# Router logits with the router as the stationary operand, turned by token in small products

## The reference

```
router_logits = x_flat @ w_router                 # 2048 x 256 times 256 x 8
top_vals, top_idx = top_k(router_logits, 2)
probs = softmax(top_vals)
h = square(relu(x_flat @ w_fc[e]));  y = h @ w_proj[e]
out = sum over the two experts e of a token of probs * y
```

## Time and profile before

| | us |
|---|---|
| median of 3 runs | 308.31 (307.42 to 308.64) |
| the profiled execution | 309.08 |
| its span | 307.3 |
| TensorE busy | 286.2 (93%), 1846 instructions |
| VectorE busy | 196.0 (64%), 467 instructions |
| ScalarE busy | 170.5 (55%), 359 instructions |
| GpSimd busy | 149.4 (49%), 132 instructions |

### The profile page before, as it was taken

The page is one execution under the profiler, slowest core; times in us unless marked ns, Lnnn a source line. Parts: engine busy times, 40 slices in busy tenths (PEclk is TensorE's granted clock), DMA queues, the critical chain, the costliest instruction groups (busy, mean ns, idle before and its releaser), DMA issues.

```text
span 307.3 us, 5659 instructions
## 1 busy us (share of the span) xinstructions
PE 286.2 (93%) x1846; PEld 253.6 (83%) x1846; DVE 196.0 (64%) x467; ACT 170.5 (55%) x359; POOL 149.4 (49%) x132
## 2 busy tenths in 40 slices
PE   5798999999899899999999998999999999799992
PEld 5787788887778789888988987989988999688881
DVE  2785999988967977865546689455546455513332
ACT  0679659797657835444666544356565555422320
POOL 3863101003472023776676687558766667637400
PEclk9799999999999999999999999999999999989998
DMA  6999980017984001244344434343444344429998
GB/s 172 360 365 377 373 323 0 0 11 208 202 213 65 0 20 36 55 69 71 53 71 69 68 57 70 53 69 55 73 69 71 63 65 65 54 33 152 192 198 282
DMA packets 33356, 36.92 MB, mean 120 GB/s; under 512 B 5168, under 2 KB 30512, under 8 KB 33296
## 3 DMA queue, kind: packets, MB, share of 16 engines
q0 software_dynamic: 13840, 17.20, 34.6%
q1 hardware_dynamic: 16560, 17.25, 16.8%
q10 hardware_dynamic: 2928, 2.10, 2.1%
HBM read 24.68 MB, written 13.96 MB: 126 GB/s over the span
## 4 chain that ended last, share of the span: by engine, by line
PE 74%; DVE 13%; ACT 6%; issue 4%; DMA 1%; POOL 0%; DVEq 0%; ACTq 0%; POOLq 0%
PE ps L366 62%; PE ps L586 5%; PE ps L434 5%; DVE cum L983 2%; ACT h L749 2%; DVE gu L1127 2%; DVE Wpj_lo L1122 2%; DMA X<-in_L_attn_x_dram 1%; DVE guT_lo L1132 1%; ACT X L695 1%; DVE h2T_lo L1003 1%; DVE gi L986 1%; PE ps L380 1%; DVE hT_lo L950 1%; DVE X L1140 1%
## 5 line engine op out<-in xcount | busy, mean ns | idle before, releaser
L1364 POOL DMA_INDIRECT xg<-xh_dram,gather_u x39 | 46.6, 1196 | 55.7 <-DVE picks L1157 46.3
L1373 POOL DMA_INDIRECT acc_dram<-yb,gather_u x39 | 62.2, 1596 | 16.4 <-issue 8.8
L366 PE MATMUL ps<-h2T_lo,Wgu_hi 128*128 128x512 f32 x128 | 43.1, 397 | 0.0
L366 PE MATMUL ps<-h2T_hi,Wgu_hi 128*128 128x512 f32 x128 | 41.1, 402 | 1.3 <-DVE h2T_lo L1003 0.9
L366 PE MATMUL ps<-h2T_hi,Wgu_lo 128*128 128x512 f32 x128 | 39.8, 392 | 0.0
L366 PE MATMUL ps<-Wd_hi,guT_hi 128*128 128x256 f32 x128 | 36.5, 285 | 3.3 <-DVE guT_lo L1132 3.3
L1127 DVE TENSOR_TENSOR gu<-gu,ps 128x512 f32<-128x512 f32 x32 | 21.9, 685 | 27.2 <-PE ps L366 25.2
L366 PE MATMUL ps<-Wd_hi,guT_lo 128*128 128x256 f32 x128 | 36.2, 283 | 0.0
L366 PE MATMUL ps<-Wd_lo,guT_hi 128*128 128x256 f32 x128 | 36.1, 282 | 0.0
L1174 DVE TENSOR_TENSOR aT_lo<-ps,aT_hi 128x256 fp32r<-128x256 f32 x39 | 16.5, 424 | 29.0 <-ACT aT_hi L797 24.8
L769 ACT ACTIVATE gu<-ps 128x512 f32<-128x512 f32 x32 | 19.0, 595 | 24.5 <-PE ps L366 23.6
(11 more groups left out here) (178 smaller groups left out, 677.2 us busy)
## 6 DMA issues: line engine op xcount, KB each, us to landing
X<-acc_dram POOLq DMA_DIRECT2D x8, 512.0 KB, 11.0
acc_dram<-zero SPq DMA_DIRECT2D x1, 2176.0 KB, 17.4
X<-in_L_attn_x_dram SPq DMA_DIRECT2D x4, 512.0 KB, 7.4
Wgu_raw<-in_L_attn_w_gate_up_dram SPq DMA_DIRECT2D x4, 512.0 KB, 9.3
Wfc_raw<-in_L_ffn_w_fc_dram SPq DMA_DIRECT2D x4, 512.0 KB, 12.5
xh_dram<-X ACTq DMA_DIRECT2D x4, 512.0 KB, 7.5
Wpj_raw<-in_L_ffn_w_proj_dram SPq DMA_DIRECT2D x4, 512.0 KB, 4.7
out_dram<-X SPq DMA_DIRECT2D x3, 512.0 KB, 5.5
```

The costliest lines, as they stand in the source:

```text
L366: return nc.tensor.matmul(dst, lhs, rhs, start=start, stop=stop, skip_group_check=group)
L1364: pool.indirect_dma_start(out=xg[i % XG][:, :], out_offset=None, in_=xh_dram, in_offset=bass.IndirectOffsetOnAxis(ap=gather_u[:, i:i + 1], ...
L1373: pool.indirect_dma_start(out=acc_dram[i % 2], in_=yb[i % YB][:, :], in_offset=None, compute_op=ALU.add, out_offset=bass.IndirectOffsetOnA ...
```

## The change

`logits(c)` now has `Wr_two` as the stationary operand and all 512 tokens of hT as the moving one: two products of 16 columns by 512 (k = 0, 1) and two of 8 by 512, in one group, 4 in all. The result is by expert: 16 partitions (hi-weight sums in the first 8, lo-weight sums in the others), 512 tokens. A new ScalarE `take_logits(c)` copies it to `by_expert` in SBUF (a place that the feed-forward uses later). A new TensorE `turn_logits(c)` multiplies, for each tile j, by_expert's 16x128 as the stationary operand by `fold` (16x8, two identities of 8 above each other), which both transposes and adds the two halves; operands are plain float32. VectorE's `take_logits(c)` copies these 128x32 to `logit`, once per chunk. All results use bank 7 from its first column, so that logits(c) waits for VectorE's copy of c-1, and ScalarE's copy of c waits for the turning of c-1. `fold` is made by one VectorE addition near the start. `top_two` waits for all four copies. Where each step stands in the queues is in the diff.

```diff
--- before.py
+++ after.py
@@ -144,6 +144,8 @@
         guT_at = room(8 * KB)
         gain = [put(f"gain{b}", [P, K, S], F32, at)
                 for b, at in enumerate((cum_at, cum_at, Wpj_hi_at + 8 * KB, Wpj_hi_at + 12 * KB))]
+
+        by_expert, fold = put("by_expert", [P, S], F32, guT_at), put("fold", [P, E], F32, guT_at + 2 * KB)
         guT = [(put(f"guT{u}_hi", [P, S], F32R, guT_at + 4 * KB * u),
                 put(f"guT{u}_lo", [P, S], F32R, guT_at + 4 * KB * u + 2 * KB)) for u in range(2)]
 
@@ -207,7 +209,9 @@
         xh_ready, xh_half = [sem(f"xh_ready{b}") for b in range(B)], sem("xh_half")
         xh_stored = [sem(f"xh_stored{b}") for b in range(B)]
         xT_done, hT_hi, hT_split, wr_hi, wr_split = sem("xT_done"), sem("hT_hi"), sem("hT_split"), sem("wr_hi"), sem("wr_split")
-        logit_done, logit_copied = sem("logit_done"), sem("logit_copied")
+        logit_done, logit_taken, logit_turned, logit_copied = (sem("logit_done"), sem("logit_taken"), sem("logit_turned"),
+                                                               sem("logit_copied"))
+        fold_ready = sem("fold_ready")
         q2_ready, q_ready = sem("q2_ready"), sem("q_ready")
         zero_row, zero_stored = sem("zero_row"), sem("zero_stored")
         x_copied = sem("x_copied")
@@ -386,15 +390,24 @@
                 pe.wait_ge(hT_split, K * (c + 1))
                 if c == 0:
                     pe.wait_ge(wr_split, 1)
+                else:
+                    pe.wait_ge(logit_copied, c)
+                for k in range(K):
+                    product(ps[0:2 * E, LOGIT, :], Wr_two[:, k, :, :].rearrange("p h e -> p (h e)"), hT[c][0][:, k, :],
+                            k == 0, False, True)
+                for k in range(K):
+                    last = product(ps[0:E, LOGIT, :], Wr_two[:, k, 0, :], hT[c][1][:, k, :], False, k == K - 1, True)
+                last.then_inc(logit_done, 1)
+
+            def turn_logits(c):
+
+                pe.wait_ge(logit_taken, c + 1)
+                if c == 0:
+                    pe.wait_ge(fold_ready, 1)
                 for j in range(J):
-                    t = J * c + j
-                    for k in range(K):
-                        rows_hi, rows_lo = (hT[c][h][:, k, j * P:(j + 1) * P] for h in range(2))
-                        product(ps[:, LOGIT, t * 2 * E:(t + 1) * 2 * E], rows_hi,
-                                Wr_two[:, k, :, :].rearrange("p h e -> p (h e)"), k == 0, False, True)
-                        last = product(ps[:, LOGIT, t * 2 * E:t * 2 * E + E], rows_lo, Wr_two[:, k, 0, :],
-                                       False, k == K - 1, True)
-                last.then_inc(logit_done, 1)
+                    last = nc.tensor.matmul(ps[:, LOGIT, j * E:(j + 1) * E], by_expert[0:2 * E, j * P:(j + 1) * P],
+                                            fold[0:2 * E, :], start=True, stop=True)
+                last.then_inc(logit_turned, 1)
 
             def aiv(b, n):
 
@@ -530,17 +543,21 @@
             logits(0)
             transpose_x(1)
             aiv(0, 4)
+            turn_logits(0)
             aiv(0, 5)
+            logits(1)
             transpose_x(2)
             aiv(1, 0)
-            logits(1)
+            turn_logits(1)
             aiv(1, 1)
+            logits(2)
             transpose_x(3)
             aiv(1, 2)
-            logits(2)
+            turn_logits(2)
             aiv(1, 3)
             logits(3)
             output_projection(0, 0)
+            turn_logits(3)
             output_projection(0, 1)
             aiv(1, 4)
             aiv(1, 5)
@@ -713,6 +730,12 @@
                 act.wait_ge(router_loaded, 16)
                 A.activation(Wr_two[:, :, 0, :], Wr[:, :, :], ACT.Copy).then_inc(wr_hi, 1)
 
+            def take_logits(c):
+                act.wait_ge(logit_done, c + 1)
+                if c:
+                    act.wait_ge(logit_turned, c)
+                A.activation(by_expert[0:2 * E, :], ps[0:2 * E, LOGIT, :], ACT.Copy).then_inc(logit_taken, 1)
+
             def decay(b, r):
                 act.wait_ge(aiv_done, 6 * b + r + 1)
                 if b == 3:
@@ -818,6 +841,7 @@
             decay(0, 1)
             normalise_x(1)
             store_xh(0)
+            take_logits(0)
             input_gate(0, 0)
             input_gate(0, 1)
             split_h(1)
@@ -826,11 +850,14 @@
             gains(0)
             normalise_x(3)
             store_xh(2)
+            take_logits(1)
             split_h(2)
             store_xh(3)
+            take_logits(2)
             split_h(3)
             decay(1, 0)
             decay(1, 1)
+            take_logits(3)
             weights_hi(3)
             input_gate(1, 0)
             input_gate(1, 1)
@@ -1004,14 +1031,13 @@
                                            in1=h2T[b % 2][0][:, k, :].bitcast(F32), op0=ALU.mult,
                                            op1=ALU.subtract).then_inc(h2T_split, 1)
 
-            def take_logits():
-                dve.wait_ge(logit_done, B)
-                two = ps[:, LOGIT, 0:2 * T * E].rearrange("p (t h e) -> p t h e", h=2, e=E)
-                chain.step(V.tensor_copy(logit[:, :, :], two[:, :, 1, :]))
-                V.tensor_tensor(logit[:, :, :], logit[:, :, :], two[:, :, 0, :], ALU.add).then_inc(logit_copied, 1)
+            def take_logits(c):
+                dve.wait_ge(logit_turned, c + 1)
+                V.tensor_copy(logit[:, J * c:J * (c + 1), :].rearrange("p t e -> p (t e)"),
+                              ps[:, LOGIT, 0:J * E]).then_inc(logit_copied, 1)
 
             def top_two():
-                dve.wait_ge(logit_copied, 1)
+                dve.wait_ge(logit_copied, B)
                 te = [P, T, E]
                 rank_te = rank8[:, None, :].to_broadcast(te)
                 work = logit
@@ -1181,6 +1207,7 @@
             split_router()
             statistics(2)
             dve.wait_ge(consts_ready, 1)
+            V.tensor_tensor(fold[0:2 * E, :], ident[0:2 * E, 0:E], ident[0:2 * E, E:2 * E], ALU.add).then_inc(fold_ready, 1)
             V.tensor_copy(lane16[:, :], lane_i[:, :])
             V.tensor_copy(token[:, :], token_i[:, :])
             chain.step(V.tensor_copy(lane[:, :], lane_i[:, :]))
@@ -1190,17 +1217,20 @@
             normalise_x(2)
             gated_value(0, 0)
             split_h(1)
+            take_logits(0)
             gated_value(0, 1)
             scales()
             signal(0, 0)
             signal(0, 1)
+            take_logits(1)
             split_h(2)
             cumulate(0, 0)
             recur(0, 0)
+            take_logits(2)
             cumulate(0, 1)
             split_h(3)
             recur(0, 1)
-            take_logits()
+            take_logits(3)
             top_two()
             add_residual(0, 0)
             add_residual(0, 1)
```

## The result

The changed kernel takes 311.94 us (median of 4 runs, 311.05 to 312.92), the kernel before 308.08 in the same comparison: ratio 1.0127, 95% interval 1.009 to 1.0164. It is 3.9 us slower; 3.2 more had been forecast, from the median of 308.31 known then to 311.5. The profiled execution took 312.02 us, its span is 310.3.

The account below looks back on a forecast made before the run. TensorE was taken as three quarters of the chain, with little room between engines at the edit. Waits making the count 3.2 us late took the profiled 309.08 to 312.3, or 311.5 us on the median; range 309.4 to 314.4.

Parts of the forecast that it names:

- The cost of a turn: TensorE, per chunk: four f32 products standing as eight instructions 0.11 us apart, 0.89 us; ends 0.24 and 1.7.
- The product part: TensorE, per chunk: 4 products with 512 moving columns take 0.91 us in place of 16 taking 1.70.
- Wait 1: TensorE waits at turn_logits(1) from 29.5 us for ScalarE's copy behind normalise_x(3); VectorE's split_h(2) ends at 33.2 instead of 32.0.
- Step 2 and 3: VectorE waits 0.7 us for turn_logits(2), with recurrence work behind it; output projection starts at 42.6 instead of 40.41 us.
- Step 4: turn_logits(3) comes behind half the projection: top_two starts at 45.6 us, +4.4; the count is at 49.95, 3.2 later.
- What arrives at the end: After the count, VectorE falls back from 4.4 us late to TensorE's lateness; everything behind ends 3.2 us late.
- rival D: The 3.2 us delay is there at 50 us but given back before 110 us: some 308.5 us; 8%.
- rival A: TensorE's clock falls at 42.6 us, slowing the projection's first half before turn_logits(3): +1.7, 313.2 us; 25%.
- one of my signs of being wrong: A granted clock of 0.50 between 40 and 50 us was listed among signs that the forecast was wrong.
- my sum: Whole kernel: profiled execution of 309.08 us plus 3.2 gives 312.3; put on the median, 0.77 lower, 311.5 us.
- Rival B: Turns are cheap, 0.03 us an instruction, or ScalarE is early: only +1.3, 309.6 us; 15%.
- Rival C: TensorE's issue time sets the end: no stop at turn_logits(1) and cheap turns give -2.2 us, 306.1; 7%.

Follow-up runs that it names:

- turn by transposes: Changed kernel with copies and last turn reordered; each turn made four transposes, VectorE adding the halves in one reduction, fold gone: 308.39 us, ratio 1.0003.
- two experiments, one at each of them: Each against the changed kernel: ScalarE's copy of chunk 1 ahead of normalise_x(3), 310.94 us; VectorE's copies of chunks 1 and 2 behind the splits, 309.61 us.
- the busy wait: Changed kernel plus 16 small keep_clock products in TensorE's queue in front of logits(3): 310.83 us, ratio 1.0089 to the kernel before.
- the products alone: Changed kernel without turns, ScalarE's copies, three of VectorE's four copies, logits(c)'s wait for the previous copy and fold; routing by meaningless logits: 308.29 us, ratio 0.9984.
- ScalarE's copy early: Changed kernel with ScalarE's take_logits(1) moved ahead of normalise_x(3): 310.94 us, ratio 1.0094 to the kernel before.
- the turns doubled: Changed kernel with the four products of each turn_logits issued twice, same result: 314.97 us, ratio 1.0203 to the kernel before.

## Why the prediction was right, point by point

Right in sign and size: +3.2 forecast, worked out on the path and put on the median of 308.31; +3.9 and +2.9 measured in two comparisons. By its steps, counted from the first product of logits(0), at 20.65 us before and 19.47 after:

- *The cost of a turn*: 0.89 us taken; 0.99 in the trace (23.72 - 22.73). The product part 0.92 (20.39 - 19.47), 0.91 taken. So TensorE's work does hardly change, by 0.2 us per chunk: page part 1 gives PE 286.2 us busy before and

```profile
PE 286.2 (92%) x1830; PEld 248.9 (80%) x1830; DVE 195.9 (63%) x470; ACT 172.7 (56%) x363; POOL 149.5 (48%) x132
```

  after. The Trainium skill (TensorE: Matmul & The Clock Gate, LDWEIGHTS) gives a load by its columns whatever its rows, an estimated 0.85 us for the eight of a turn. The f32 products agree with that roughly (0.99 us for the eight, 0.12 apart at 16 rows, where the old products with 128 rows were 0.11 apart); the transposes of the later experiment do not, being 0.35/4 = 0.09 us apart with 128 columns loaded, under the estimated 0.107 of the rule. There the measurement decides.
- *Wait 1*: turn_logits(1) forecast 10.0 us after logits(0), found 9.8; its wait of 0.71 (about 1 forecast) and the delay of split_h(2) are shown by two experiments, one at each of them.
- *Step 2 and 3*: the copy of chunk 2 waits 0.87 (0.7 forecast); the projection comes 21.75 us after logits(0), 21.95 forecast.
- *Step 4*: top_two at 24.95 forecast, 26.63 found; the count at 29.3 forecast, 30.96 found. Both misses are the clock: in the profile of the busy wait, at full clock, they are 45.74 - 20.75 = 24.99 and 29.31.
- *What arrives at the end*: all of it at equal clock. VectorE's larger lateness at top_two was lost again before 73.63 us, as forecast, and at 114.47 us the lateness is still that of the count. So rival D, by which it is given back before 110 us, did not come.

What I did not have: rival A, put at 25% as an alternative, came on top of the forecast in both profiles of the changed kernel. A granted clock of 0.50 between 40 and 50 us was also one of my signs of being wrong, and it is there; what is right is the account of the waits, not one of the clock. In the medians it hardly shows, since clock falls elsewhere vary as well: at 12 to 13 us in 5 of the 13 profiles of all kernels, between 37 and 45 us in 3, between 266 and 277 us in 9. That the profiled execution, 312.02, came so near to the 312.3 of my sum is luck: the fall at 41 us (+1.65) and the slower end (+0.75) stand against falls at 12 us (1.2) and 268 us (1.35) that the profile of before had and this one had not. My sum came near the median partly because the falls come out about even on the two kernels (mean clock 0.992 in both); the forecast of the waits is what the equal-clock figures (+3.4, +3.2 against 3.2) and the stretch (+3.24) confirm. Rival B (cheap turns) was wrong for f32 products and came nearer for transposes, 0.35 us a turn where it took 0.24. Rival C was refuted by the turn by transposes, which has both of its conditions (no wait at turn_logits(1), a turn of 0.35 us) and is no faster than before, and by the products alone: not even free turns collect more than about 1 us.

## What to carry to other kernels

A producer and a consumer inserted into in-order queues cost what stands behind them: two copies of 0.19 us, put ahead of work that did not need them, cost 1.6 to 2 us, and moving them was worth more than making the turn three times cheaper. Before saving an engine's time in a stage, take out all the new work at no price and look what then waits; here the 3.2 us of saved products were worth under 1. And where executions differ by their clock, compare stretches between two events of the trace, not spans. A fit to equal clock helps with the rest, but it hides what a kernel does to its own clock.

## What the runs showed of the hardware

- An f32 product with 16 rows and 8 moving columns stands as two instructions, 0.12 us apart, 0.24 together (changed kernel); a transpose of the same operand as one, 0.09 us (turn by transposes).
- ScalarE's copy of 16x512 from PSUM took 0.57 to 0.59 us, one of 128x512 0.57: the partitions left idle saved nothing. TensorE's product with 16 stationary columns took the 0.23 us of one with 128 (0.46 for two, 19.47 to 19.93; 0.228 in the earlier trace rows).
- The granted clock fell to 0.50 as the projection began at 41 us, after waits of 1.60 and 0.75 us with 0.9 us of products between; with waits of 1.62 and 0.75 it stayed at 1.00 in the profile of ScalarE's copy early, in which it had fallen at 13 us, and in that of the turns doubled (1.62 and 0.76), in which it had not. When it falls is not fixed by the kernel alone; what else decides it was not tried. A fall was worth 1.2 us at 12, 1.65 at 41 and 1.35 at 268.
